# Loading expert weights earlier: a finer down-projection ring and gate/up loads pushed one chunk ahead

## The reference

```python
mod = (silu(c) @ wmod).reshape(4, 6, 1, -1)        # sa, ca, ga, sb, cb, gb
h = layernorm(x) * (1 + ca) + sa
x = x + clamp(ga) * attn(h, W_Q, W_K, W_V, W_O)
h = layernorm(x) * (1 + cb) + sb
# 8 experts (H = 1024, top 2), and a shared one (HS = 2048) with a sigmoid gate
x1 = silu(einsum('td,ehd->teh', h, w_gate))
x3 = einsum('td,ehd->teh', h, w_up)
expert_out = einsum('teh,edh->ted', x1 * x3, w_down)
routed = einsum('te,ted->td', comb, expert_out)
shared = silu(h @ sh_gate.T) * (h @ sh_up.T) @ sh_down.T
x = x + clamp(gb) * (routed + sigmoid(h @ se_gate_w.T) * shared)
```

## Time and profile before

| | us |
|---|---|
| median of three runs | 5055.93 |
| the three runs | 4823.11, 5081.66, 5055.93 |
| the profiled execution | 4817.25 |
| its span on the slowest core | 4815.7 |
| spans of the eight cores | 4792.8 to 4815.7 |

### The profile page before, as it was taken

How to read it: one execution, slowest core, us unless ns; L and a number is a source line. 1 busy time by engine, 2 the same in 40 slices (tenths; PEclk the granted TensorE clock), 3 DMA queues, 4 the chain that set the end, 5 groups by cost and what they waited for, 6 DMA issues and landing times.

```text
span 4815.7 us, 48375 instructions; the slowest of 8 cores (4792.8 to 4815.7 us)
## 1 busy us (share of the span) xinstructions
PE 3529.5 (73%) x14970; PEld 1423.9 (30%) x14970; DVE 1183.4 (25%) x2423; ACT 678.7 (14%) x1156; POOL 409.6 (9%) x779
## 2 busy tenths in 40 slices
PE   3425777777777777777743597887979888797886
PEld 1222222222222222222432243333434333343332
DVE  0374222222222222222106111212122121211212
ACT  0242222222222222221013100000000000000000
POOL 1000000000000000000110111111111101111010
PEclk8657777777777776777855798998989899898998
DMA  9712000000000010101560544353433425334353
GB/s 202 132 70 44 14 14 14 14 14 14 14 14 14 14 16 14 20 14 27 80 95 0 87 73 72 51 76 50 67 61 55 74 39 88 53 53 72 51 80 94
DMA packets 112809, 246.64 MB, mean 51 GB/s; under 512 B 13889, under 2 KB 14018, under 8 KB 110274
## 3 DMA queue, kind: packets, MB, share of 16 engines
q0 software_dynamic: 109696, 209.92, 27.9%
q1 hardware_dynamic: 2882, 33.63, 1.9%
HBM read 444.94 MB, written 8.39 MB: 94 GB/s over the span
## 4 chain that ended last, share of the span: by engine, by line
PE 37%; DMA 7%; DVE 2%; issue 2%; POOL 1%; ACT 1%; DVEq 0%; ACTq 0%; POOLq 0%
PE pdn L1199 12%; PE px L1092 12%; PE px L1117 11%; DMA rB<-wmodB 2%; DMA rD<-wd 2%; DMA rA<-wg 2%; POOL rD L100 1%; PE pm L289 1%; DVE h L417 1%; DMA rA<-shg 0%; DMA rD<-shd 0%; DVE t1f L409 0%; DVE t1f L412 0%; DVE ysb L1131 0%; PE px L943 0%
## 5 line engine op out<-in xcount | busy, mean ns | idle before, releaser
L1092 PE MATMUL px<-h,rA 128*128 128x512 bf16 x2560 | 591.7, 391 | 161.5 <-DMA rA<-wg 125.6
L1199 PE MATMUL pdn<-ysb,rD 128*128 128x512 bf16 x2560 | 583.3, 392 | 159.6 <-DMA rD<-wd 116.0
L542 PE MATMUL pacc<-h_full,rA 128*128 128x512 bf16 x2560 | 606.7, 398 | 31.7 <-DMA rA<-wk 19.4
L1117 PE MATMUL px<-h,rA 128*128 128x512 bf16 x2560 | 565.6, 379 | 0.0
L1199 PEld LDWEIGHTS pdn<-ysb,rD 128*128 128x128 bf16 x2560 | 255.6, 100 | 485.8 <-issue 204.2
L1092 PEld LDWEIGHTS px<-h,rA 128*128 128x128 bf16 x2560 | 255.6, 100 | 484.1 <-issue 201.2
L1131 DVE TENSOR_TENSOR ysb<-x1s,px 128x1024 bf16<-128x1024 bf16 x80 | 97.7, 1221 | 1197.6 <-PE px L1117 1197.6
L542 PEld LDWEIGHTS pacc<-h_full,rA 128*128 128x128 bf16 x2560 | 257.7, 102 | 367.9 <-issue 98.5
L1209 DVE SCALAR_TENSOR_TENSOR x_own<-pdn,gbcl,x_own 128x512 f32<-128x512 f32 x320 | 240.3, 751 | 498.8 <-PE pdn L1199 498.8
L1117 PEld LDWEIGHTS px<-h,rA 128*128 128x128 bf16 x2560 | 250.5, 98 | 302.0
L1106 ACT ACTIVATE x1s<-px 128x1024 bf16<-128x1024 f32 x80 | 81.9, 1024 | 1772.3 <-PE px L1092 1772.3
(11 more groups left out here) (156 smaller groups left out, 2583.1 us busy)
## 6 DMA issues: line engine op xcount, KB each, us to landing
rD<-wd POOLq DMA_DIRECT2D x128, 256.0 KB, 8.2
rA<-wg POOLq DMA_DIRECT2D x128, 256.0 KB, 5.1
rA<-wu POOLq DMA_DIRECT2D x128, 256.0 KB, 4.9
rB<-wmodA POOLq DMA_DIRECT2D x48, 512.0 KB, 10.0
rB<-wmodB POOLq DMA_DIRECT2D x96, 256.0 KB, 5.5
xl<-ximg SPq DMA_DIRECT2D x16, 1024.0 KB, 4.9
rA<-wk POOLq DMA_DIRECT2D x32, 256.0 KB, 4.4
rA<-wq POOLq DMA_DIRECT2D x32, 256.0 KB, 4.3
```

Of the source, the lines that this page charges most:

```text
L542: t.matmul(pacc[:, bank * 512:bank * 512 + 512], ub[:, (dc % 8) * 128:(dc % 8) * 128 + 128], moving_fn(dc, qtr), start=(dc == 0), stop=(dc ...
L1092: lambda t, ub=ub, dc=dc, half=half: t.matmul(px1[:, half * 512:half * 512 + 512], ub[:, (dc % 8) * 128:(dc % 8) * 128 + 128], h2[:, dc * ...
L1117: lambda t, ub=ub, dc=dc, half=half: t.matmul(px3[:, half * 512:half * 512 + 512], ub[:, (dc % 8) * 128:(dc % 8) * 128 + 128], h2[:, dc * ...
L1199: t.matmul(pdn[rot][:, :], ub[:, dloc * 128:dloc * 128 + 128], ysb[:, hc * 1024 + th * 512: hc * 1024 + th * 512 + 512], start=(hc == 0), ...
```

## The change

Three things change. The down ring gets twice as many slots of half the width, and the down projection goes in quarters of 64 matmuls with eight units of 512 columns each; quarter q + 1 is pushed before the matmuls of quarter q are written, and quarter 0 of the next expert behind the last quarter's matmuls. The gate and up units of a chunk are pushed at the end of the chunk before, and those of an expert's first chunk at the end of the last chunk of the expert before, so ahead of the row loads and the down quarters 1 to 3. For expert 0 the gate and up units of its first chunk are pushed ahead of the expert loop and its row loads, and its down quarter 0 in chunk 6.

```diff
-    ringD = Ring(em, es3, "rD", 9, 1024, BF16)
+    ringD = Ring(em, es3, "rD", 18, 512, BF16)
...
+    def push_gu(e2, hc2):
+        gu = []
+        for proj in range(2):
+            us = []
+            for half in range(2):
+                if e2 >= NE:
+                    dten = d_shg if proj == 0 else d_shu
+                    srcp = dten[(e2 - NE) * 8 + hc2, :, half * 1024:half * 1024 + 1024]
+                else:
+                    dten = d_wg if proj == 0 else d_wu
+                    srcp = dten[e2, hc2, :, half * 1024:half * 1024 + 1024]
+                us.append(ringA.push(srcp))
+            gu.append(us)
+        return gu
+
+    gu_pend = [push_gu(0, 0)]
+    dpre_next = {0: None}
...
-        def push_down(half, e=e, shared=shared):
+        def push_down(q, e=e, shared=shared):
             us = []
             for hc in range(HC):
                 if shared:
-                    srcap = d_shd[(e - NE) * 8 + hc, :, half * 1024:half * 1024 + 1024]
+                    srcap = d_shd[(e - NE) * 8 + hc, :, q * 512:q * 512 + 512]
                 else:
-                    srcap = d_wd[e, hc, :, half * 1024:half * 1024 + 1024]
+                    srcap = d_wd[e, hc, :, q * 512:q * 512 + 512]
                 us.append(ringD.push(srcap))
             return us
         dpre = {}
-        dpre[0] = push_down(0)
+        if dpre_next.get(0) is not None:
+            dpre[0] = dpre_next[0]
+            dpre_next[0] = None
...
-            gu = []
...
-                    us.append(ringA.push(src))
-                gu.append(us)
+            gu = gu_pend[0]
+            if hc == HC - 2 and dpre.get(0) is None:
+                dpre[0] = push_down(0)
...
             ringA.consumed(gu[1][0][0])
             ringA.consumed(gu[1][1][0])
+            nxt = (e, hc + 1) if hc < HC - 1 else (e + 1, 0)
+            if nxt[0] < NEU:
+                gu_pend[0] = push_gu(nxt[0], nxt[1])
...
-        for half in range(2):
-            if half == 1:
-                dpre[1] = push_down(1)
-            dunits = dpre[half]
-            for dloc in range(8):
-                doc = half * 8 + dloc
+        for q in range(4):
+            if q < 3:
+                dpre[q + 1] = push_down(q + 1)
+            elif e + 1 < NEU:
+                dpre[0] = None
+            dunits = dpre[q]
+            for dloc in range(4):
+                doc = q * 4 + dloc
...
             for u in dunits:
                 ringD.consumed(u[0])
+            if q == 3 and e + 1 < NEU:
+                def push_down_next(e2=e + 1):
...
+                        us.append(ringD.push(srcap))
+                    return us
+                dpre_next[0] = push_down_next()
```

More of the change, by code:

```diff
@@ L1072, in build_nc @@
                     v_gbcl[0] = em.mark("vector")
-            gu = []
-            for proj in range(2):
-                us = []
-                for half in range(2):
[L1077 to L1082, removed]
-                    us.append(ringA.push(src))
-                gu.append(us)
+            gu = gu_pend[0]
+            if hc == HC - 2 and dpre.get(0) is None:
+                dpre[0] = push_down(0)
             w1_ = [gu[0][0][2], gu[0][1][2], h2_done]
@@ L1215, in build_nc @@
                 ringD.consumed(u[0])
+            if q == 3 and e + 1 < NEU:
+                def push_down_next(e2=e + 1):
+                    us = []
+                    for hc in range(HC):
+                        if e2 >= NE:
+                            srcap = d_shd[(e2 - NE) * 8 + hc, :, 0:512]
+                        else:
+                            srcap = d_wd[e2, hc, :, 0:512]
+                        us.append(ringD.push(srcap))
+                    return us
+                dpre_next[0] = push_down_next()
         gx["x1s"] = em.mark("vector")
```

## The result

The changed kernel's median is 4508.4 us over ten runs. Against the kernel before, on the same chip, the ratio is 0.9344, with a 95% interval from 0.9332 to 0.9355; the forecast was 4491.8 us and 0.932. The profiled execution took 4511.4 us.

The account below looks back on a forecast made before the run. TensorE was taken to bound the kernel, idling 303.5 us for expert weights behind GpSimd's in-order load queue. -303.5 - 43 - 17 + 26 + 12 = -325.5 from 4817.25 gave 4491.8 us, ratio 0.932, range 4440 to 4755.

Parts of the forecast that it names:

- The waits, -303.5: TensorE's waits for gate weights at expert starts and down weights inside each down projection all go: -303.5 us.
- the second place: Expert starts: gate-weight waits (125.6 + 33.6 us) go because next gate and up units stand in the queue before quarter 1.
- Slow starts, -43: Low-clock starts after the waits go: 22.4 us in ten second down halves, 20.5 us in nine first gates.
- Start of expert 0, -17: Before expert 0's first modulation matmul: eight down units no longer precede the modulation loads, which land earlier, -17 us.
- The new wait in expert 0, +26 and +12: Expert 0's modulation loads fall behind up pairs: 3.7 us in each of 7 chunks, +26; slow gates and modulation matmuls, +12.
- Ring D at no cost: Down projection: half-size units pushed a quarter ahead land in time, costed at 0, with 50 us kept for the range.
- the floor of 0.85: Down loads: lowest price of a half-size unit, half that of a 256 KB unit, 0.85 us; 1.0 was taken.
- the ceiling of 1.94: Down loads: highest price of a half-size unit if the price per transfer doesn't shrink, 1.94 us.
- A fixed price per load: Rival: ring D's stall returns in small pieces at the quarters, 4500 to 4542 us; inside the forecast's own 0.78.
- Only one of the stalls goes: Rival: for example the in-order queue holds quarters back and the down stall stays, 4659 us; chance 0.05.
- The clock: Rival: dense expert matmuls get a lower granted clock, up to 4751 us, chance 0.12; beyond it up to 4914, 0.03.

Follow-up runs that it names:

- experiment 2: Kernel before with only the gate and up units pushed a chunk ahead, ring D still nine wide slots in halves: 4737.2 us in one execution.
- Experiment 1: Changed kernel with gate and up units pushed at the head of their chunk, as before, so down quarters alone: 4466.9 us, ratio 0.9235 to the kernel before.
- Experiment 4: Experiment 3 with row broadcasts behind quarters 0 and 1 and two blocks' eighth-chunk matmuls last: 4428.8 and 4433.3 us, ratio 0.9159; repeated, 4437.3 us, 0.919.
- Experiment 3: Changed kernel, but expert 0's gate and up units of chunks 1 to 7 pushed at their old place: 4466 to 4474 us, ratio 0.9238.
- experiment 8: Changed kernel with ring D as 36 slots of 256 columns and the down projection in eighths: ratio 0.9341 to the kernel before.
- experiment 5: Changed kernel with expert 0's down quarter 0 pushed at its old place, ahead of the first modulation loads: 4510.5 us in one execution.
- experiment 6: Kernel before with its down ring as 18 slots of 512 columns, still filled and freed in halves: 4896.5 us in one execution.
- experiment 7: Experiment 6 with the units' waits only before the first group of a half: no ratio; four cores of the profiled execution spanned 4844 to 4892 us.

## Why the prediction was right, and where its steps were off

**The waits, -303.5.** Right in sum and in both places. For the second place the prediction gave the credit to the wrong part. It said that at an expert's start the waits go because the gate and up units now stand ahead of the down quarters. That order does work: in experiment 2 the first gate waits for nothing, though 28 us of the 159 come back a chunk later. But it isn't needed. Experiment 1 has these units behind the quarter, and the waits go all the same (6.1 us left). What the queue's order did before, the quarters undo by themselves, as the units that block it are let go a quarter earlier. The sum came out right because it doesn't depend on which of the two does it. I had worked out the landing of quarters 1 to 3 by this very count and not applied it to the gate pair.

**Slow starts, -43.** The second halves' and first gates' share came. But I wrote that the short gap "stays, and what it costs in clock with it". It stayed at 3 us, yet its cost rose: three of ten first halves began at the lower clock in the profile before, eight of ten projections do after, 5 x 1.7 = 8.5 us. On the six cores whose down matmuls are all in the trace, it is one to three of ten before and seven to nine after. Of the 6.6 us by which this part missed, this is all and a little more. Experiment 4 shows it to be the gap's; why the same gap lets the clock fall more often after the change stays open.

**Start of expert 0, -17.** 14.8: the modulation pair landed 7.7 us after its issue (2693.39 to 2701.12 us), where I had counted 5.4, so TensorE still waits 4.54 us.

**The new wait in expert 0, +26 and +12.** The eleven waits sum to 25.7 us, but split otherwise than worked out: 2.65 to 4.53 for the first pair of a chunk (2.5 was forecast), 0.7 or nothing for the second (1.2). The slow gates cost 62.1 - 52.7 = 9.4 us (8.5 forecast), and the slow modulation matmuls 26.4 - 18.5 = 7.9, where I had put "a little": 17 in all for 12. Experiment 3 gives the whole of it, 40 us with the waits, to the order of the loads.

**Ring D at no cost.** Right, also at twice the loads (experiment 8). A half unit costs 0.84 us at the head of a queue (experiment 5), at the floor of 0.85 and not at the ceiling of 1.94; I had taken 1.0.

**The rivals.** A fixed price per load is refuted by experiments 6 and 8. The Trainium skill (DMA: Bandwidth & Descriptors, Anatomy of one DMA) gives 2.0 us fixed for each transfer. As one transfer's latency the rows leave room for it (3.4 us for 64 KB from issue to landing); as a price of each of several it doesn't hold, as they overlap: 0.84 us for 128 KB. "Only one of the stalls goes" is refuted by the changed kernel. The clock didn't take the gain back: it is 1.00 over 100 us without a gap. The Trainium skill (TensorE: Matmul & The Clock Gate, Part 1) has a die at 13/16 of the clock when three or more of its cores run dense matmuls together; the profiled execution doesn't show that, with 1.00 on all eight cores from 3800 to 3900 us.

So the forecast of 4491.8 was 16.6 us low: about 7 behind expert 0's gate and up chunks, where the slow starts of the down projections alone cost 8.5, 6 in those chunks, and the rest within the spread of the cores ahead of them.

## What to carry to other kernels

When a ring has barely more slots than one block of work takes, an engine stands at the end of each block, and an in-order load queue spreads that to loads whose own slots are free. Free and refill in smaller blocks first: here that alone gave the whole gain, and moving other loads ahead cost 40 us where a third ring's loads fell behind them. For every push that is moved ahead, ask which release it waits for, and what stands behind it in the same queue.

## What the hardware showed that I hadn't expected

- Waits in front of an instruction aren't free in number: 17 before each group of eight matmuls made 128 matmuls take 31.79 us instead of 27.79, while nine showed nothing (experiments 6 and 7). An engine that has waited for a semaphore once needn't wait again for the same value.
- A gap of 3 us with two small matmuls inside was enough to bring the clock of the next matmuls down to 1.2 GHz, in three of ten cases in one kernel and eight of ten in another, 1.7 us each time. Without the broadcasts in it the gap did the same, and with the gap closed no down projection started slowly.
- Splitting loads in two, and again in two, cost about 0.02 to 0.03 us of a DMA engine for each added packet (experiment 8).
